# Lightning attention: the mixing product on the full array, with a block-diagonal matrix that VectorE writes in two parts

## The chip, the core and the metric

The kernel runs on one core of a Trainium2 chip. The metric is the time of one execution on the device, in microseconds (us), as the median of several runs. The core has a matrix engine (TensorE; PE in the profile, and PEld for its weight loads, which overlap the products), VectorE (DVE), ScalarE (ACT), GpSimd (POOL), and SyncE (SP), which issues the DMAs of this kernel. TensorE multiplies a stationary matrix (the weights, at most 128 rows by 128 columns) by a moving one that streams through it.

## The reference

Two decoder layers run on 2048 tokens (32 sequences of 64) of width 256. The change touches one of their six blocks, the lightning attention of the second layer, cut here to what is computed for each of 16 heads:

```python
qkv = silu(x @ w_qkv.T)                     # split into q, k, v of 128 each
for each block of 32 tokens, in order:
    o_inter = (q * q_decay) @ kv
    o_intra = ((q @ k.T) * diag_decay) @ v
    kv = block_decay * kv + (k * k_decay).T @ v
out = norm_w * out * rsqrt(mean(out * out) + eps)
return (sigmoid(x @ w_gate.T) * out) @ w_out.T
```

A sequence has 64 tokens only, so for each sequence and head this is one 64x64 matrix: the scores q k^T times a decay that is zero above the diagonal, applied to v. The kernel computes it in that form.

## The kernel before

`build` runs the blocks of both layers one after the other, with a barrier between stages. `lightning_attention` first normalises the tokens (`layernorm`, which leaves them split into a high and a low half-precision part, `xh` and `xl`), and then runs 64 steps: 16 heads (h) times four blocks (q) of 512 tokens, or eight sequences. In a step s the work is this:

- TensorE (the function under `@block.tensor`, `pair`): `wide` makes Q and K of the next step (6 products of 512 columns each, into banks 0 and 1). Then come the **scores** of this step (L1867): for each of the four tiles of 128 tokens (two sequences) and each of its two halves r, one product of k and q of the same sequence, in full precision, 128 rows by 64 columns of the array, 64 columns streamed, into bank 4. Then `wide` for the gate of the next step, `output` of the step before (12 products of 256 columns, from `yh` and `yl`), the **mixing** (L1880), and `values` of the next step (24 products of 128 columns). The mixing has eight products in full precision: the values `vS` of one sequence as weights (64 rows by 128 columns, so half of the array's rows), and the masked scores of that sequence `A[half[r], j, :]`, 64 columns, streamed. Half r writes to bank 4 + r, columns 256 to 511.
- VectorE: `mask` multiplies the scores in bank 4 by the decay and writes `A` (L1758, one instruction of 128x256), `add` sums the output of the step before from banks 6 and 7 into `ACC` (L1769), `gated` makes y (L1775) and, after ScalarE's `yh`, its low part `yl` (L1778). In the first step of each head `weights_low` (L1626) stands between `add` and `gated`.
- ScalarE: takes Q, K, gate and values out of their banks, copies the result of the mixing into `oS` (L1725, from both banks), and makes `yh` (L1732). GpSimd sums the squares of `oS`, and splits the weights of a later block.

The order on each engine is written out by hand, and semaphores join them: `scored` and `masked` between TensorE and VectorE, `mixed` and `ocopied` between TensorE and ScalarE. The scores wait for `ocopied` of the step before, because bank 4 holds a part of the mixing's result. `prep` lets ScalarE begin, and TensorE after it, once VectorE has prepared its constants (L1748 to L1752). Each full-precision product appears in the trace as two weight loads and two products, so the eight of a step are 16 rows.

Of the kernel before, what the change touches and what calls it, by code (L numbers as in the profile page):

```python
# [20 lines left out]
ALU = mybir.AluOpType  # L21
ACT = mybir.ActivationFunctionType
AX = mybir.AxisListType.X
ds = bass.ds

BATCH, SEQ, D = 32, 64, 256
TOK = BATCH * SEQ
P = 128
# [4 lines left out]
TPB = BLK // P  # L33
# [547 lines left out]
def gqa_cross_attention(nc, m, w, W):  # L581
# [13 lines left out]
    with ExitStack() as own:  # L595
# [22 lines left out]
        NLOAD = 1 + 2 + 1 + 1 + 3 + 2  # L618
        NPREP = 1 + KC * C + 1
        def preload(sp):  # L620
# [853 lines left out]
class KeptWeights:  # L1474
# [24 lines left out]
    def parts(self, h):  # L1499

        A, B, D2 = self.views(self.WS[:, :])[h]
        return ((A, self.W13[:, :, :, 0:P]), (B[:, :, :, 0:self.FB], self.W13[:, :, :, P:]), (D2, self.W2[:, :, :]))

# [37 lines left out]
def lightning_attention(nc, m, w, KW):  # L1541
# [18 lines left out]
    with ExitStack() as own:  # L1560
        def sb(n, s, dt=F32):
            return m.sb("d_" + n, s, dt, own)
# [7 lines left out]
        tri = sb("tri", [P, SEQ])  # L1570
        decay = sb("decay", [P, NH, SEQ])
        qT, kT, gt, vS, oS = (sb(n, [P, 2, BLK]) for n in ("qT", "kT", "gt", "vS", "oS"))
        A = sb("A", [P, TPB, SEQ])
        half = [slice(r * SEQ, (r + 1) * SEQ) for r in range(2)]
        y = sb("y", [P, BLK])
        yh, yl = (sb(n, [P, BLK], F16) for n in ("yh", "yl"))
# [4 lines left out]
        eps = sb("eps", [P, 1])  # L1581
        sd = sb("sd", [P, NT])
        rstd = sb("rstd", [P, NT])
        NPREP = 4
        EVENLY, LATELY = 2, [(0, 1), (0, 3), (1, 1)]

        def flat(x):
# [42 lines left out]
        with nc.Block() as block:  # L1630
# [45 lines left out]
            @block.scalar  # L1676
            def _(act):
                act.wait_ge(prep, NPREP)
                act.sem_inc(evac, 4)  # L1679
                act.sem_inc(ocopied, 1)  # L1680
                act.sem_inc(squared, 4)

                def weights_high(h):

                    act.wait_ge(wload, 48 * h + 48)
                    act.wait_ge(wt_in, 16 * h)
                    act.activation(flat(Ws[:, 0]), flat(Wn[:, :, :]), ACT.Copy, scale=SPLIT).then_inc(whigh, 1)

                def qk(s, q):
                    for n, dst in enumerate((qT, kT)):  # L1690
                        act.wait_ge(proj, 4 * s + n + 1)
                        act.activation(dst[:, q % 2, :], m.bank[n][:, :], ACT.Silu, scale=UNSPLIT).then_inc(evac, 1)

                def gate(s, q):
                    act.wait_ge(proj, 4 * s + 3)
                    act.activation(gt[:, q % 2, :], m.bank[2][:, :], ACT.Tanh, scale=0.5 * UNSPLIT).then_inc(evac, 1)

                def values(s, q):
                    act.wait_ge(proj, 4 * s + 4)
                    act.activation(vS[:, q % 2, :], m.bank[3][:, :], ACT.Silu, scale=UNSPLIT).then_inc(evac, 1)  # L1700

                def root(tiles):
                    act.wait_ge(ssq, tiles.stop // TPB)
                    act.activation(sd[:, tiles], m.bank[0][:, tiles], ACT.Sqrt, scale=UNSCALE / (NH * HD),
                                   bias=eps[:, :]).then_inc(sd_ready, 1)

                def pair(i, last):
                    for st in range(SPP):
                        u, q = divmod(st, SPH)
                        s, h = i * SPP + st, i * 2 + u  # L1710
                        end = last and st == SPP - 1
                        if not end:
                            qk(s + 1, q + 1)
                            if q == 0 and not (last and u == 1):
                                weights_high(h + 1)
                            if last and (u, q) in LATELY:
                                KW.scalar(act, NH - 2 + LATELY.index((u, q)))
                            elif not last and q == EVENLY:
                                KW.scalar(act, h)
                            gate(s + 1, q + 1)  # L1720
                        else:
                            root(slice(0, NT - TPB))
                        act.wait_ge(squared, 2 * s + 2)
                        act.wait_ge(mixed, s + 1)
                        act.activation(oS[:, q % 2, :].rearrange("p (j r t) -> p j r t", j=TPB, r=2),  # L1725
                                       m.psum[:, 4:6, 256:512].rearrange("p r (j t) -> p j r t", j=TPB),
                                       ACT.Copy).then_inc(ocopied, 1)
                        if not end:
                            values(s + 1, q + 1)
                        act.wait_ge(yready, s + 1)  # L1730
                        m.wait_apart(act, outs, s + 1)
                        act.activation(yh[:, :], y[:, :], ACT.Copy, scale=nw[:, ds(h, 1)]).then_inc(yhigh, 1)  # L1732
                        if end:
                            root(slice(NT - TPB, NT))

                for h in range(NH):
                    act.activation(decay[:, h, :], rel[:, :], ACT.Exp, scale=slope[:, h:h + 1]).then_inc(decays, 1)
                qk(0, 0)
                gate(0, 0)
                values(0, 0)  # L1740
                act.sem_inc(outs, 1)
                with act.Fori(0, PAIRS - 1) as i:
                    pair(i, False)
                pair(PAIRS - 1, True)

            @block.vector
            def _(dve):
# [2 lines left out]
                dve.wait_ge(loaded, 16 * 4)  # L1750
                dve.tensor_scalar(nw[:, :], nw[:, :], 0.5 * YS, None, ALU.mult).then_inc(prep, 1)
                dve.tensor_scalar(slope[:, :], slope[:, :], -1.0, None, ALU.mult).then_inc(prep, 1)  # L1752
                dve.sem_inc(masked, 1)
                dve.sem_inc(summed, 1)

                def mask(s, h):
                    dve.wait_ge(scored, s + 1)
                    dve.tensor_tensor(A[:, :, :], m.bank[4][:, 0:256].rearrange("p (a b) -> p a b", a=TPB),  # L1758
                                      decay[:, ds(h, 1), :].broadcast_to((P, TPB, SEQ)), ALU.mult).then_inc(masked, 1)

                def add(s, q, fresh):
                    dve.wait_ge(outs, s + 2)
# [51 lines left out]
            def _(pe):  # L1814
# [35 lines left out]
                def pair(i, first, last):  # L1850
                    for st in range(SPP):
                        u, q = divmod(st, SPH)
                        s, h = i * SPP + st, i * 2 + u
                        end = last and st == SPP - 1
                        nslot, nq = ((st + 1) // SPH) % 2, (q + 1) % SPH
                        if not end:
                            if nq == 0:
                                pe.wait_ge(wt_in, 16 * (h + 2))
                            wide(s + 1, nq, nslot, Q)
                            wide(s + 1, nq, nslot, K)  # L1860
                        pe.wait_ge(evac, 4 + 4 * s + 2)
                        pe.wait_ge(masked, s + 1)
                        pe.wait_ge(ocopied, s + 1)
                        for j in range(TPB):
                            for r in range(2):
                                tok = slice(j * P + r * SEQ, j * P + (r + 1) * SEQ)
                                mm = pe.matmul(m.bank[4][half[r], j * SEQ:(j + 1) * SEQ], kT[:, q % 2, tok], qT[:, q % 2, tok],  # L1867
                                               start=True, stop=True)
                        mm.then_inc(scored, 1)
                        if not end:  # L1870
                            wide(s + 1, nq, nslot, GT)
                        else:
                            square_sums(range(SPH - 1))
                        if not (first and st == 0):
                            output(s - 1, (st - 1) % SPP // SPH)
                        pe.wait_ge(masked, s + 2)
                        pe.wait_ge(evac, 4 + 4 * s + 4)
                        for j in range(TPB):
                            for r in range(2):
                                mm = pe.matmul(m.bank[4 + r][:, 256 + j * SEQ:256 + (j + 1) * SEQ],  # L1880
                                               vS[half[r], q % 2, j * P:(j + 1) * P], A[half[r], j, :], start=True, stop=True)
                        mm.then_inc(mixed, 1)
                        if not end:
                            values(s + 1, nq, nslot)
# [402 lines left out]
def experts_top4(nc, m, w, KW, rows_dram, y_dram, out):  # L2287
# [20 lines left out]
    with ExitStack() as own:  # L2308
# [25 lines left out]
        with nc.Block() as block:  # L2334
# [179 lines left out]
            def _(pe):  # L2514
                def hidden(s, weights, rows):
# [4 lines left out]
                    for j in range(len(weights)):  # L2520
                        tok, (A, B) = slice(j * BLK // len(weights), (j + 1) * BLK // len(weights)), weights[j]
                        for bank, W in ((0, lambda x, k: A(x, k, 0)), (1, lambda x, k: A(x, k, 1)), (2, B)):
# [148 lines left out]
```

## Time and profile before

| | us |
|---|---|
| median of 3 runs | 2389.93 |
| lowest and highest of them | 2388.23, 2400.44 |
| the profiled execution, its own time | 2389.24 |
| its span, from first to last instruction | 2387.4 |
| mean granted TensorE clock | 0.769 |
| lightning attention's 64 steps, first to last mixing | 651.3 to 1179.3 |

Three kinds of view are read below. A table of stretches gives each engine's busy time in a piece of the span, with the TensorE clock that was granted (1.00 is full speed, 2.4 GHz, and 0.50 is 1.2 GHz). Groups of instructions give count, busy time and mean duration. The timeline lists instructions in order of time, with like ones merged: a row with x16 and 1.11 us is sixteen instructions, from the start of the first to the end of the last. The recorded duration of a product holds the way through the array too, so the pace of a row is read from starts: its length less the duration of one, divided by the count less one.

### The profile page before, as it was taken

What the parts mean: (1) busy time and instruction counts of PE and PEld (TensorE: products, weight loads), DVE (VectorE), ACT (ScalarE), POOL (GpSimd) and SP (SyncE); (2) the same over time, 40 slices, a digit from 0 to 9 for tenths busy, and PEclk for the clock granted to TensorE, in tenths of its full rate; (3) what the DMA queues carried; (4) which work ended last, traced back from release to release, by engine and by line L of the source; (5) the groups of instructions that cost most, each with busy time, mean ns of one, the idle gap of its engine ahead of it and who ended that gap; (6) DMA issues with size and microseconds to landing.
All of it is one profiled execution on the core that took longest, in us unless ns stands there. A gap on an engine that the chain in (4) does not pass through costs nothing. (4 is left out here: it accounts for less than half of the span.)

```text
span 2387.4 us, 43105 instructions
## 1 busy us (share of the span) xinstructions
PE 1657.3 (69%) x15916; PEld 1021.4 (43%) x15916; DVE 1641.9 (69%) x2837; ACT 1285.0 (54%) x1770; POOL 1184.8 (50%) x1087
## 2 busy tenths in 40 slices
PE   6874595288499999999874566666666654178761
PEld 3332364265266666666563122222222223157640
DVE  5999477435545555555587899999999984634344
ACT  4664485032355555555432788888888871045430
POOL 0000284244234444444434688888888880055436
PEclk9997798599699999999987555555555557589985
DMA  3000221484322332222100466565556551688844
GB/s 106 1 0 0 54 75 40 101 201 118 72 80 66 86 82 67 74 76 75 54 27 0 76 107 109 106 110 105 108 107 107 107 98 35 230 190 211 167 110 131
DMA packets 506355, 219.08 MB, mean 92 GB/s; under 512 B 425485, under 2 KB 493653, under 8 KB 506197
## 3 DMA queue, kind: packets, MB, share of 16 engines
q1 hardware_dynamic: 494677, 185.47, 34.9%
q0 software_dynamic: 11520, 31.47, 5.5%
q8 instruction: 103, 1.69, 0.3%
q14 instruction: 55, 0.45, 0.1%
HBM read 79.87 MB, written 36.31 MB: 49 GB/s over the span
## 5 line engine op out<-in xcount | busy, mean ns | idle before, releaser
L2140 POOL CAST xnT<-xl 128x2048 bf16<-128x2048 uint8 x256 | 483.5, 1889 | 15.3
L2178 PE MATMUL psum<-e_KT,e_QT 48*128 48x512 bf16 x1024 | 265.0, 617 | 251.3 <-DVE ctxT L2211 124.7
L2211 DVE TENSOR_SCALAR_CACHE_REDUCE ctxT<-psum,e_nsq 128x1024 f32<-128x1024 f32 x256 | 314.7, 1282 | 7.9 <-PE psum L2178 6.5
L2211 DVE TENSOR_SCALAR_CACHE_REDUCE e_Smore<-psum,e_nsq 128x1024 f32<-128x1024 f32 x256 | 314.7, 1282 | 1.7 <-issue 0.4
L2229 ACT ACTIVATE xh<-ctxT,e_ebias 128x2048 uint8<-128x2048 f32 x128 | 256.2, 2002 | 53.6 <-POOL e_ebias L2147 53.6
L2229 ACT ACTIVATE xh<-e_Smore,e_ebias 128x2048 uint8<-128x2048 f32 x128 | 256.2, 2002 | 42.4 <-POOL e_ebias L2147 42.4
L1653 POOL TENSOR_TENSOR d_sq<-d_oS 128x512 f32<-128x512 f32 x60 | 93.4, 1557 | 273.6 <-ACT d_oS L1725 273.6
L120 PE MATMUL psum<-xh,d_T 128*128 128x512 f16 x768 | 220.2, 382 | 5.1 <-ACTq L1679 5.1
L2178 PEld LDWEIGHTS psum<-e_KT,e_QT 48*128 48x128 bf16 x1024 | 33.9, 107 | 381.2 <-DVE ctxT L2211 190.0
L661 POOL TENSOR_TENSOR b_bias<-b_alibi,b_neg 128x1024 f32<-128x1024 f32 x16 | 37.8, 2366 | 277.5 <-DVE b_Vbd L760 277.5
L2392 POOL DMA_INDIRECT xnT<-kept_rows,f_token x96 | 95.0, 989 | 153.1 <-DVE f_token L1135 68.6
L2188 PEld LDWEIGHTS psum<-e_Vi,xnT 128*128 128x128 bf16 x4096 | 119.6, 105 | 112.2 <-issue 91.0
L1769 DVE TENSOR_TENSOR d_ACC<-psum,d_ACC 128x512 f32<-128x512 f32 x120 | 77.3, 686 | 129.9 <-PE psum L120 129.9
L2188 PE MATMUL psum<-e_Vi,xnT 128*128 128x16 bf16 x4096 | 131.4, 175 | 7.4 <-POOL xnT L2140 7.4
L120 PE MATMUL psum<-f_Z,f_W 128*128 128x256 f16 x864 | 107.0, 287 | 41.5 <-DMA f_Z<-xnT 38.5
L1778 DVE SCALAR_TENSOR_TENSOR d_yl<-d_y,d_nw,d_yh 128x512 f16<-128x512 f32 x64 | 83.6, 1306 | 74.3 <-ACT d_yh L1732 74.3
L120 PE MATMUL psum<-xl,d_T 128*128 128x512 f16 x384 | 115.1, 382 | 0.0
L120 PEld LDWEIGHTS psum<-f_Z,f_W 128*128 x864 | 86.8, 102 | 60.8 <-issue 46.6
L2147 POOL TENSOR_SCALAR e_ebias<-e_mn 128x1 f32<-128x1 f32 x256 | 73.3, 286 | 64.0 <-DVE ctxT L2211 28.6
L2555 PE MATMUL psum<-f_W,f_hh 128*128 (+1 forms) x448 | 71.0, 286 | 41.9 <-DVE f_hh L2458 36.8
L2412 ACT ACTIVATE f_Z<-psum 128x512 f32<-128x512 f32 x28 | 16.7, 597 | 152.5 <-PE psum L120 152.5
L120 PEld LDWEIGHTS psum<-xh,d_T 128*128 128x128 f16 x768 | 67.6, 98 | 71.8 <-issue 7.7
(387 smaller groups left out, 3971.4 us busy)
## 6 DMA issues: line engine op xcount, KB each, us to landing
kept_y<-ctxT SPq DMA_DIRECT2D x24, 512.0 KB, 4.6
kept_w<-k_WS SPq DMA_DIRECT2D x17, 640.0 KB, 3.5
f_W<-kept_w SPq DMA_DIRECT2D x17, 640.0 KB, 11.5
kept_y<-c_y SPq DMA_DIRECT2D x12, 512.0 KB, 4.6
d_Wn<-in_L_attn_w_qkv SPq DMA_DIRECT2D x16, 384.0 KB, 3.5
k_W<-in_L_ffn_w_routed SPq DMA_DIRECT2D x32, 176.0 KB, 3.7
kept_rows<-xnT SPq DMA_DIRECT2D x8, 512.0 KB, 3.5
xl<-xh SPq DMA_TRANSPOSE x256, 3.0
```

The costliest lines, as they stand in the source:

```text
L120: mm = pe.matmul(out, lhsT(a, k), rhs(b, k), start=(n == 0), stop=(n == len(terms) - 1))
L1653: pool.tensor_tensor(sq[:, :], o, o, ALU.mult).then_inc(squared, 1)
L1769: last = dve.tensor_tensor(a2, m.bank[6 + half][:, :], a2, ALU.add)
L1778: dve.scalar_tensor_tensor(yl[:, :], y[:, :], nw[:, ds(h, 1)], yh[:, :], ALU.mult, ALU.subtract).then_inc(ysplit, 1)
L2140: pool.tensor_copy(PT[:, sl, :], P8[:, sl, :, :].rearrange("p c q -> p (c q)").bitcast(U8)).then_inc(unpacked, 1)
L2147: pool.tensor_scalar(ebias[:, sl:sl + 1], mn[:, sl, 0:1], mn[:, sl, 1:2], LN255, ALU.min, ALU.add).then_inc(biased, 1)
L2178: mm = pe.matmul(m.bank[pair_banks(c + odd) + q], QT[rows, n // 2, :], KTt[rows, n % H // 2, col:col + BLK], start=True, stop=True)
L2188: mm = pe.matmul(m.bank[6 + j // 8][:, j % 8 * HD:(j % 8 + 1) * HD], PT[:, n % SLOTS, k // 2 * 2 * P + k % 2:(k // 2 + 1) * 2 * P:2], Vi[: ...
L2211: dve.tensor_scalar(S32[sl][:, hf * HALF:(hf + 1) * HALF].rearrange("p (a b) -> p a b", a=2), m.psum[:, b:b + 2, :], nsq[:, n + odd:n + od ...
L2229: act.activation(e8[:, sl, :], S32[sl], ACT.Exp, bias=ebias[:, sl:sl + 1], scale=-1.0, accum_out=esum[:, n:n + 1]).then_inc(exped, 1)
L2392: pool.indirect_dma_start(got[:, qd % GOT, j, :], None, rows_dram[:, :], bass.IndirectOffsetOnAxis(R.token[:, i:i + 1], 0)).then_inc(fetch ...
L2555: mm = pe.matmul(m.bank[y_bank(s) + j // 2][:, (j % 2) * D:(j % 2 + 1) * D], a, b, start=(n == 0), stop=(n == len(terms) - 1))
```

## The change

`A` becomes 128 columns wide for each tile (`[P, TPB, P]`). Its two off-diagonal blocks are set to zero once, before the first step (two more instructions counted in `prep`, so NPREP is 6). `mask` writes the two diagonal blocks, in two instructions of 64 partitions each. The mixing is four products of 128x128 by 128 columns instead of eight on half the rows, all into bank 5, and ScalarE copies that one bank. TensorE's wait for `ocopied` moves from ahead of the scores to ahead of the mixing. The scores stay as they are.

```diff
-        A = sb("A", [P, TPB, SEQ])
+        A = sb("A", [P, TPB, P])
...
-        NPREP = 4
+        NPREP = 6
...
-                        act.activation(oS[:, q % 2, :].rearrange("p (j r t) -> p j r t", j=TPB, r=2),
-                                       m.psum[:, 4:6, 256:512].rearrange("p r (j t) -> p j r t", j=TPB),
-                                       ACT.Copy).then_inc(ocopied, 1)
+                        act.activation(oS[:, q % 2, :], m.bank[5][:, :], ACT.Copy).then_inc(ocopied, 1)
...
+                for rows, other in (half, half[::-1]):
+                    dve.memset(A[rows, :, other], 0.0).then_inc(prep, 1)
...
                 def mask(s, h):
                     dve.wait_ge(scored, s + 1)
-                    dve.tensor_tensor(A[:, :, :], m.bank[4][:, 0:256].rearrange("p (a b) -> p a b", a=TPB),
-                                      decay[:, ds(h, 1), :].broadcast_to((P, TPB, SEQ)), ALU.mult).then_inc(masked, 1)
+                    for rows in half:
+                        ins = dve.tensor_tensor(A[rows, :, rows], m.bank[4][rows, 0:256].rearrange("p (a b) -> p a b", a=TPB),
+                                                decay[rows, ds(h, 1), :].broadcast_to((SEQ, TPB, SEQ)), ALU.mult)
+                    ins.then_inc(masked, 1)
...
                         pe.wait_ge(evac, 4 + 4 * s + 2)
                         pe.wait_ge(masked, s + 1)
-                        pe.wait_ge(ocopied, s + 1)
                         for j in range(TPB):
...
                         pe.wait_ge(masked, s + 2)
                         pe.wait_ge(evac, 4 + 4 * s + 4)
+                        pe.wait_ge(ocopied, s + 1)
                         for j in range(TPB):
-                            for r in range(2):
-                                mm = pe.matmul(m.bank[4 + r][:, 256 + j * SEQ:256 + (j + 1) * SEQ],
-                                               vS[half[r], q % 2, j * P:(j + 1) * P], A[half[r], j, :], start=True, stop=True)
+                            tok = slice(j * P, (j + 1) * P)
+                            mm = pe.matmul(m.bank[5][:, tok], vS[:, q % 2, tok], A[:, j, :], start=True, stop=True)
                         mm.then_inc(mixed, 1)
```

On TensorE, in the second step of the stage, the order around the mixing was this (`d_yh` and `d_yl` are the output's operands, `d_A` and `d_vS` the mixing's, `d_T` with `xh` or `xl` the values'; the size is the moving operand's, or that of the result's tile):

```order
 L120 MATMUL psum<-d_T,d_yh 128x256 x2
 L120 MATMUL psum<-d_T,d_yl 128x256
-L1880 MATMUL psum<-d_A,d_vS 128x64 [waits b_maxed,b_exped]
-L1880 MATMUL psum<-d_A,d_vS 128x64 x7
+L1882 MATMUL psum<-d_A,d_vS 128x128 [waits b_pt,b_maxed,b_exped]
+L1882 MATMUL psum<-d_A,d_vS 128x128 x3
 L120 MATMUL psum<-d_T,xh 128x128 [waits b_maxed]
 L120 MATMUL psum<-d_T,xh 128x128 x3
```

Eight products with 64 columns each have become four with 128, the neighbours on both sides are the same, and the mixing's first instruction has a third wait. (The names of semaphores are those of an earlier stage that used the same ones: `b_pt` is `ocopied`.)

On VectorE, at the start of the stage and in its first step, before:

```order
478 L1748 MEMSET d_ones 128x1
479 L1749 MEMSET d_eps 128x1
480 L1751 TENSOR_SCALAR d_nw<-d_nw 128x16
481 L1752 TENSOR_SCALAR d_slope<-d_slope 128x16
482 L1801 TENSOR_TENSOR d_decay<-d_decay,d_tri 128x1024
483 L1758 TENSOR_TENSOR d_A<-psum,d_decay 128x256
484 L1626 SCALAR_TENSOR_TENSOR d_Ws<-d_Wn,d_Ws 128x1280
```

The same place now:

```order
478 L1746 MEMSET d_ones 128x1
479 L1747 MEMSET d_eps 128x1
480 L1749 TENSOR_SCALAR d_nw<-d_nw 128x16
481 L1750 TENSOR_SCALAR d_slope<-d_slope 128x16
482 L1752 MEMSET d_A 64x4x64 x2
483 L1803 TENSOR_TENSOR d_decay<-d_decay,d_tri 128x1024
484 L1759 TENSOR_TENSOR d_A<-psum,d_decay 64x4x64 x2
485 L1626 SCALAR_TENSOR_TENSOR d_Ws<-d_Wn,d_Ws 128x1280
```

Two memsets stand ahead of ScalarE's release, and each mask is two instructions; nothing else has moved.

## Rows read from the trace of the kernel before

**Rows 1.** A stretch: PE, PEld, DVE, ACT, POOL busy (count), clock, DMA share, GB/s.

```profile
900.00:1000.00 100.00, 100.00 (x1030) 67.32 (x1030) 50.87 (x64) 53.56 (x90) 44.22 (x33) 1.00 0.29 77
```

**Rows 2.** Who waited for whom, TensorE, 640 to 1190: total us, times, longest.

```profile
PE psum L120 <- DVE d_yl L1778: 3.1, 1, 3.1
```

**Rows 3.** Timeline of TensorE, 902.9 to 905: start, us, engine, line, names, count.

```profile
902.87 0.38 PE L120 MATMUL psum<-d_T,d_yh 128*128 128x256 f16 x2
903.09 0.27 PE L120 MATMUL psum<-d_T,d_yl 128*128 128x256 f16 x1
903.29 1.11 PE L1880 MATMUL psum<-d_A,d_vS 64*128 64x64 f32 x16
904.33 0.40 PE L120 MATMUL psum<-d_T,xh 128*128 128x128 f16 x4
...
903.29 0.97 PEld L1880 LDWEIGHTS psum<-d_A,d_vS 64*128 64x128 f32 x16 [0.21 <-issue]
```

**Rows 4.** The next step's mixing, and one line's durations (ns, minimum/median/maximum), TensorE.

```profile
911.69 1.11 PE L1880 MATMUL psum<-d_A,d_vS 64*128 64x64 f32 x16
...
L1880 PEld LDWEIGHTS psum<-d_A,d_vS x1024: 182/188/188, 651.3 to 1180.1; 64*128 64x128 f32 x171
L1880 PE MATMUL psum<-d_A,d_vS x1024: 272/272/320, 651.3 to 1180.1; 64*128 64x64 f32 x171
```

**Rows 5.** Full-array full-precision weight loads, timeline of TensorE in the last step.

```profile
1175.19 2.84 PE L1847 MATMUL psum<-d_ones,d_SQ 128*128 128x1 f32 x24
1177.89 0.38 PE L120 MATMUL psum<-d_T,d_yh 128*128 128x256 f16 x2
...
1175.19 2.75 PEld L1847 LDWEIGHTS psum<-d_ones,d_SQ 128*128 128x128 f32 x24
```

**Rows 6.** Full-array products of other stages, timeline of TensorE.

```profile
346.29 1.04 PE L816 MATMUL psum<-ident,b_S 128*128 128x128 f32 x8
...
1219.63 2.75 PE L2080 MATMUL psum<-e_Wkv,ctxT 128*128 128x256 f32 x12
...
1240.21 0.62 PE L2092 MATMUL psum<-e_identb,e_Tk 128*128 128x128 bf16 x8 [0.17 <-POOL e_Tk L1980]
1240.66 0.87 PE L2080 MATMUL psum<-e_Wq,xnT 128*128 128x256 f32 x3
...
1240.61 0.19 PEld L2080 LDWEIGHTS psum<-e_Wq,xnT 128*128 128x128 f32 x1
```

**Rows 7.** VectorE groups: busy us, mean ns, idle us before and releaser.

```profile
L1758 DVE TENSOR_TENSOR d_A<-psum,d_decay 128x256 f32<-128x256 f32 x64 | 27.0, 422 | 28.6 <-PE psum L1867 28.6
...
L2449 DVE TENSOR_TENSOR f_Z<-psum,f_Z 48x512 f32<-48x512 f32 x28 | 19.5, 695 | 0.9
L2447 DVE TENSOR_TENSOR f_Z<-psum,f_Z 128x512 f32<-128x512 f32 x28 | 19.4, 691 | 107.6 <-ACT f_Z L2412 107.5
```

**Rows 8.** Timeline of VectorE around the start of a head, and TensorE's next output.

```profile
920.20 1.29 DVE L1769 TENSOR_TENSOR d_ACC<-psum,d_ACC 128x512 f32<-128x512 f32 x2 [2.16 <-PE psum L120]
921.41 1.48 DVE L1626 SCALAR_TENSOR_TENSOR d_Ws<-d_Wn,d_Ws 128x1280 f16<-128x1280 f32 x1
...
925.41 0.75 DVE L1778 SCALAR_TENSOR_TENSOR d_yl<-d_y,d_nw,d_yh 128x512 f16<-128x512 f32 x1 [1.07 <-ACT d_yh L1732]
...
927.09 0.38 PE L120 MATMUL psum<-d_T,d_yh 128*128 128x256 f16 x2
...
L1778 DVE SCALAR_TENSOR_TENSOR d_yl<-d_y,d_nw,d_yh x64: 750/1595/1597, 655.1 to 1182.7; 128x512 f16<-128x512 f32 x64
```

**Rows 9.** The stage's start: timeline of VectorE, GpSimd, TensorE, and a memset elsewhere.

```profile
636.57 2.09 DVE L1752 TENSOR_SCALAR d_slope<-d_slope 128x16 f32<-128x16 f32 x1
...
638.55 0.57 POOL L1506 MEMSET k_W<- 128x512 f32 x1
...
638.86 0.58 PE L120 MATMUL psum<-xh,d_T 128*128 128x512 f16 x1 [5.14 <-ACTq L1679]
...
L336 DVE MEMSET a_pad<- 96x192 f32 x1 | 0.2, 218 | 2.6 <-PEq L179 2.6
```

## The prediction

> **What bounds the kernel now.** Only the lightning attention changes, so I read its stretch alone. The table of stretches comes first [rows 1]: in 100 us of it TensorE is busy for all 100, at full clock, while VectorE has 51, ScalarE 54 and GpSimd 44. The view of who waited for whom [rows 2] confirms it: from 640 to 1190 us TensorE's products waited for another engine once that it shows, for 3.1 us, at the stage's end. The timeline gives the period: mixings start at 903.29 and 911.69, so a step takes 8.40 us [rows 3, 4], and 62 of the 63 spacings are the same (the last, without a next step's products, is shorter). So TensorE alone sets the time of the 64 steps, and what the change does to TensorE's own sequence is what it does to the kernel, as long as the others keep up.
>
> How long does the mixing take there? The last product before it starts at 903.09 and the first after it at 904.33 [rows 3]. The three output products from 902.87 stand 0.11 apart, so the last would have made room after 0.11. The mixing's slot is 904.33 - 903.09 - 0.11 = 1.13 us. Inside it, the weight loads come in pairs, one for each half of the rows, and their row is 0.97 us for 16 of 0.188 [rows 3, 4]: (0.97 - 0.19) / 7 = 0.111 us per pair. The streaming of 64 columns is shorter than that and lies under the loads: the pace is that of loading 128 columns of full-precision weights, 8 pairs x 0.111 = 0.89. The other 0.24 are the edges: 0.09 before the first load (903.29 against 903.20), and what lies between the last product, which starts at 903.29 + 1.11 - 0.27 = 904.13, and 904.33, of which its pair's own streaming is the smaller part. TensorE stands empty while it goes over to half arrays, and again while it comes back.
>
> **TensorE's mixing after the change.** Four products of two weight loads each make 8 loads in place of 8 pairs. The trace has such loads on the full array, those of the square sums: 24 loads and products, whose load row is 2.75 us with 0.19 for one, (2.75 - 0.19) / 23 = 0.111 [rows 5]. So a full load costs what a pair of half ones did. New is that each load's product streams 128 columns, twice as many. Full-precision products of 128 columns come at (1.04 - 0.27) / 7 = 0.11 [rows 6], but these are transposes, with a cheaper load; products of 256 columns come at (2.75 - 0.38) / 11 = 0.215, and their loads, which are of the expensive kind, hide entirely [rows 6]. So load and product run side by side, and with both at 0.11 the pace should be 0.112: 8 x 0.112 = 0.90 us.
>
> The edges go. From a 16-bit product to full precision on the full array the trace shows products at 1240.66 and a load at 1240.61, directly behind the last one of L2092: that row ends at 1240.83 and one lasts 0.22, so the last starts at 1240.61 too, and no empty time lies between [rows 6]. On the way back, the 24 products from 1175.19 to 1177.89 take 2.70 / 24 = 0.1125 each, the step to the output's first 16-bit product included [rows 5]. Here the mixing's first load has a 256-column output product of 0.11 to hide under. So the slot is 0.90 in place of 1.13, and from the unrounded starts I take 0.238 us per step; 64 x 0.238 = **15.2 us less**. Bounds: a pace of 0.109 instead of 0.112 gives 0.262, or 16.8; a first load that doesn't hide costs 0.107 per step, which leaves 0.131, or 8.4. I take 15.2, since the row at 1240.61 shows the load going ahead.
>
> The Trainium skill, in "TensorEngine Tiling (Array Packing)", section Key Properties, says that changing the tiling mode drains TensorE; by that rule both edges are drains and the change removes two of the four per step. The trace agrees, with 0.09 us ahead of the mixing.
>
> **The waits.** The wait for `ocopied` goes from the scores to the mixing. The copy that it asks for belongs to the step before, and is 7 us old by then; nothing is queued behind it that it holds. The scores lose a wait that never held either. TensorE's queue reads such waits ahead, as it did at 1240.61, where a load with a wait of its own directly follows L2092's last product [rows 6].
>
> **VectorE's mask.** Time goes by elements per partition and not by partitions: 48x512 took 695 ns and 128x512 691 [rows 7]. So each half of the mask costs the 422 ns of the whole one [rows 7], and VectorE has 64 x 0.42 = 27 us more work. It is hidden where the mask stands: VectorE was idle for the 2.16 us between the mask and `add` at 920.20 [rows 8], and the mixing that needs `A` starts at 903.29 + 2 x 8.40 = 920.09, 2.05 us after the mask's end. Without that cover it would cost 0.42 per step.
>
> **What is late next.** The tightest place is `yl` in a head's first step, where `weights_low` (1.48 us) stands behind `add`: it ends at 925.41 + 0.75 = 926.16, and TensorE needs it at 927.09, so 0.93 is left [rows 8]. `add` starts when the output is ready, and a mixing shorter by 0.24 brings the next output nearer by as much: 0.69 stays. But `yl` takes 0.75 or 1.6 us [rows 8], by what GpSimd does beside it. Should it fall on the long one there, 0.85 - 0.69 = 0.16 us would be missing in 15 steps, 2.4 us at most. Nothing at the low end. I take 0.
>
> **The stage's start.** ScalarE, and after it TensorE (638.86), wait for VectorE's constants, which end at 636.57 + 2.09 = 638.66 [rows 9]. Two memsets of 256 elements per partition are added there; one of 192 took 218 ns [rows 9], so about 0.27 each, 0.5 us in all, once. If GpSimd's memset (638.55 to 639.12) held them up [rows 9], it would be 1.0; 0 if they ran into each other. I take 0.5.
>
> **Sum.** 0.5 - 15.2 = -14.7. The profiled execution took 2389.24 (its span 2387.4 and 1.84 around it), which gives 2374.5, and a span of 2372.7. The median of the runs shown stands 0.7 above it, at 2389.93: 2375.2. The period of a step is 8.16 in place of 8.40. The later stages begin after a barrier and should only move forward; I allow them 2 us either way, about what the two lower runs differ by.
>
> **Rivals.**
> 1. Load and product don't overlap when both are 0.11 long (slower). For: no row shows an expensive load with a product of 128 columns. Against: in half arrays and under 256 columns they overlap entirely. Then each of the 8 costs 0.107 more, at worst: 8 x 0.107 - 0.238 = +0.62 per step, 40 us, 2430. It decides from a pace of 1.13 / 8 = 0.142 us per load: above that the change loses.
> 2. Two half products at once are worth more than I say (slower). What half arrays save is streaming: 8 pairs of 64 columns against 8 of 128. One 64-column pass pair is half of the 0.107, so 0.43 us per step would be lost if streaming set the pace on both sides, 27 us, 2417. Against it stands the pace of 0.111 per pair, which is twice what 64 columns need [rows 3, 4]. The Trainium skill has this as a rule, in "TensorE: Matmul & The Clock Gate", section Packing small matmuls: products with few rows, put into different row groups, run at once, and that is their gain. By it alone the change would be a loss.
> 3. The edges stay (no change). If the empty time came from going between 16-bit and full precision, or from the waits, and not from half arrays, both would stay, and the mixing's inner part is as long as before: 0.5 us more at the start, 2390.5. Against it stand both edges of [rows 5, 6].
> 4. The first load doesn't hide: -8.4 + 0.5, 2382.
> 5. The change doesn't do what it says because VectorE takes TensorE's place as the bound: at 51 of 100 busy plus 5 it is far from that; it could only be the place named above, +2.4, which is 2377.6 and in the forecast's own range.
>
> **How the numbers follow.** Forecast (2371 to 2380) 0.79; first load exposed 0.07; edges stay 0.05; no overlap 0.05; streaming sets the pace 0.03; something below 2371 0.01. The range reaches from 2371 to the exposed load, 2382, and leaves out 0.14. A measurement of this kernel tells 0.5%, 12 us, from no change, so the border is 2378: faster by more is the forecast but for a small part of it where the start, `yl` and the later stages add up, 0.76; within 0.5% are that part, the exposed load and the edges, 0.16; slower 0.08.
>
> **What would show it.** Right: mixings 8.16 us apart; the mixing's product row eight strong and about 0.8 us from its first start to its last; nothing empty at either side, with the first product 0.11 behind the last output product; each mask two rows of 0.42; TensorE's idle before `d_yh` as before; TensorE's first product of the stage at about 639.4. Wrong: loads at over 0.12 us (rival 1 or 2); 0.09 and more ahead of the mixing (3 or 4); TensorE idle on `d_yl` in the second step of each head (`yl` late); a later stage that took back more than 2 us.

## The result, and the profile after

| | before | after |
|---|---|---|
| median of 13 runs each, taken side by side, us | 2398.05 | 2379.80 |
| lowest of them | 2386.53 | 2374.46 |
| ratio, with its 95% interval | | 0.9939 (0.9918 to 0.9961) |
| profiled execution, its own time | 2389.24 | 2379.82 |
| its span | 2387.4 | 2378.0 |

The change makes the kernel 0.6% faster: 14.6 us by the ratio, with 9 to 20 as its interval. The medians lie further apart, 18.3 us; the ratio is that of the means, in which one run of before, 2484.98 in a slower state, is left out. A second comparison on another occasion, with six runs of the changed kernel and 17 of the one before, gave 0.9932 (0.9916 to 0.9948). The medians themselves sit higher than the three runs of before that stood ahead of the prediction: over 13 runs before is at 2398, not at 2390.

The stretch of the same length as in [rows 1], then TensorE's waits in the stage from its first products on, as in [rows 2], both of the changed kernel:

```profile
900.00:1000.00 100.00, 100.00 (x967) 69.78 (x965) 58.96 (x77) 55.42 (x94) 45.34 (x33) 1.00 0.28 77
...
PE psum L120 <- DVE d_yl L1780: 3.1, 1, 3.1
PE psum L120 <- ACT d_qT L1692: 0.7, 1, 0.7
```

TensorE is still busy for all 100 us at full clock, and is still the only bound; VectorE has gone from 51 to 59. The 3.1 us at the stage's end are what they were. The 0.7 us, once and at the start of the stage, don't stand in the first trace of before, but they are not the change's: the third trace of before has such a wait of 0.3, and the third of after has none. They go with the moment at which the clock rises, which the section on the start takes up. The timeline of TensorE around a mixing answers to [rows 3] (the mixing is L1882 now):

```profile
900.08 0.38 PE L120 MATMUL psum<-d_T,d_yh 128*128 128x256 f16 x2
900.29 0.27 PE L120 MATMUL psum<-d_T,d_yl 128*128 128x256 f16 x1
900.30 0.97 PEld L1882 LDWEIGHTS psum<-d_A,d_vS 128*128 128x128 f32 x8
900.40 1.06 PE L1882 MATMUL psum<-d_A,d_vS 128*128 128x128 f32 x8
...
901.30 0.39 PE L120 MATMUL psum<-d_T,xh 128*128 128x128 f16 x4
...
908.55 1.06 PE L1882 MATMUL psum<-d_A,d_vS 128*128 128x128 f32 x8
```

The first load starts with the last output product (900.30 against 900.29), so it lies under it; the first product of the mixing is 0.11 behind that one, where it was 0.20; eight loads take 0.97, which is (0.97 - 0.19) / 7 = 0.111 each; and the values' products begin 0.90 after the mixing's first, where it was 1.04. The next mixing starts at 908.55, 8.15 us later, where it was 8.40. Of the 0.25 us, 0.09 went ahead of the mixing, 0.15 inside it and at its back, and 0.01 in the first of the values' products.

VectorE in a head's first step answers to [rows 8]:

```profile
914.32 0.86 DVE L1759 TENSOR_TENSOR d_A<-psum,d_decay 64x256 f32<-64x256 f32 x2 [0.39 <-PE psum L1868]
916.90 1.29 DVE L1771 TENSOR_TENSOR d_ACC<-psum,d_ACC 128x512 f32<-128x512 f32 x2 [1.73 <-PE psum L120]
918.11 1.48 DVE L1626 SCALAR_TENSOR_TENSOR d_Ws<-d_Wn,d_Ws 128x1280 f16<-128x1280 f32 x1
919.51 1.53 DVE L1777 SCALAR_TENSOR_TENSOR d_y<-d_gt,d_oS 128x512 f32<-128x512 f32 x1
922.12 0.75 DVE L1780 SCALAR_TENSOR_TENSOR d_yl<-d_y,d_nw,d_yh 128x512 f16<-128x512 f32 x1 [1.08 <-ACT d_yh L1730]
```

The mask is two instructions and 0.86 us long, and 1.73 us of idle time are still left between it and `add`. `yl` keeps its short form here.

### The profile page after: what moved, and what is told of

It reads as the page before. It is cut to its first block and busy times, and to the rows that moved or that the text cites. A ratio compares the mean times of both kernels' runs of the same rounds, so it can differ in the third digit from the quotient of the medians.

```text
span 2378.0 us, 42208 instructions
## 1 busy us (share of the span) xinstructions
PE 1652.0 (69%) x15404; PEld 1027.5 (43%) x15404; DVE 1673.6 (70%) x2903; ACT 1286.5 (54%) x1770; POOL 1188.3 (50%) x1087
```

## Is the mask really free?

> The kernel before with one edit: the mask is written by two instructions of 64 partitions, as in the change, while the mixing stays on half arrays. Theory (VectorE's extra 0.42 us lies under TensorE's products): 128 mask instructions of 0.42 us, mixings still 8.40 us apart, time as before within 0.5%. Rival (VectorE's cover is gone somewhere, so the change paid for its mask and would have gained more without it): a step of 8.40 to 8.82, up to 27 us slower.

```diff
                 def mask(s, h):
                     dve.wait_ge(scored, s + 1)
-                    dve.tensor_tensor(A[:, :, :], m.bank[4][:, 0:256].rearrange("p (a b) -> p a b", a=TPB),
-                                      decay[:, ds(h, 1), :].broadcast_to((P, TPB, SEQ)), ALU.mult).then_inc(masked, 1)
+                    for rows in half:
+                        ins = dve.tensor_tensor(A[rows, :, :], m.bank[4][rows, 0:256].rearrange("p (a b) -> p a b", a=TPB),
+                                                decay[rows, ds(h, 1), :].broadcast_to((SEQ, TPB, SEQ)), ALU.mult)
+                    ins.then_inc(masked, 1)
```

Measured: ratio to before 0.9991 (0.9970 to 1.0011). In its trace, one mask of VectorE and two mixings of TensorE:

```profile
907.13 0.86 DVE L1759 TENSOR_TENSOR d_A<-psum,d_decay 64x256 f32<-64x256 f32 x2 [0.37 <-PE psum L1869]
...
901.32 1.11 PE L1882 MATMUL psum<-d_A,d_vS 64*128 64x64 f32 x16
...
909.72 1.11 PE L1882 MATMUL psum<-d_A,d_vS 64*128 64x64 f32 x16
```

The mask costs 0.42 us more and the step stays at 8.40. So VectorE's part of the change is free, and what the step gained came from TensorE's own sequence.

## What sets the pace of the mixing: load or streaming?

Two runs of the changed kernel alter how many columns each product of the mixing streams, and neither computes the right result. The first leaves out half of each output tile, and besides the line shown it zeroes bank 5 once, ahead of the first step. The second writes overlapping pieces. Each ran once, so its trace is what counts.

> The changed kernel, whose mixing streams only the first 64 of A's 128 columns per product (the other half of each output tile is left out, so half of the result isn't computed; the bank is zeroed once). Theory (the loading of full-precision weights sets the pace, 0.112 us per load, and streaming lies under it): the mixing still takes 8 x 0.112, the step 8.10 to 8.15. Rival 2 (streaming sets the pace on the full array): each of 8 passes 0.053 shorter, a step of 7.72, 27 us less over the stage.

```diff
-                            mm = pe.matmul(m.bank[5][:, tok], vS[:, q % 2, tok], A[:, j, :], start=True, stop=True)
+                            mm = pe.matmul(m.bank[5][:, j * P:j * P + SEQ], vS[:, q % 2, tok], A[:, j, 0:SEQ], start=True, stop=True)
```

> The changed kernel, whose mixing streams 192 columns per product instead of 128, into overlapping pieces of the bank (a wrong result, the same number of products). Theory (load and streaming run side by side, the longer one sets the pace): 192 columns need 0.160 us, so the pace is 0.162, the mixing 1.30 instead of 0.90, the step 8.55, which is 0.15 above the kernel before: the break-even pace is 0.142. Rival 1 (load and streaming add): 0.27 per pass, a step of 9.4.

```diff
+                            cols = slice(min(j * P, BLK - 192), min(j * P, BLK - 192) + 192)
-                            mm = pe.matmul(m.bank[5][:, tok], vS[:, q % 2, tok], A[:, j, :], start=True, stop=True)
+                            mm = pe.matmul(m.bank[5][:, cols], vS[:, q % 2, tok], A[:, :, :].rearrange("p a b -> p (a b)")[:, cols],
+                                           start=True, stop=True)
```

Timeline of TensorE, first of the run with 64 columns, then of the one with 192; in each the mixing, the product behind it, and the next mixing:

```profile
900.91 1.00 PE L1883 MATMUL psum<-d_A,d_vS 128*128 128x64 f32 x8
901.75 0.39 PE L120 MATMUL psum<-d_T,xh 128*128 128x128 f16 x4
...
909.01 1.00 PE L1883 MATMUL psum<-d_A,d_vS 128*128 128x64 f32 x8
```

```profile
906.84 1.47 PE L1883 MATMUL psum<-d_A,d_vS 128*128 128x192 f32 x8
908.14 0.39 PE L120 MATMUL psum<-d_T,xh 128*128 128x128 f16 x4
...
915.39 1.47 PE L1883 MATMUL psum<-d_A,d_vS 128*128 128x192 f32 x8
```

With half the columns the mixing takes 0.84 in place of 0.90 and the step is 8.10 (8.097 as the median of all): only the last product's own streaming is saved, the seven others come at the pace of their loads. With half as many again it takes 1.30, or 0.163 per pass, and the step is 8.56, above the kernel before. So both go side by side, the longer one counts, and at 128 columns the two are of nearly one length. That refutes rival 2, for which 64 columns would have given 7.72, and rival 1, for which 192 would have given 9.4; and it puts the change on the good side of the break-even pace of 0.142.

## What are the edges?

Two runs put one more product ahead of the mixing, on half of the rows or on all of them. Its result is overwritten. Each ran once.

> The changed kernel with one further product on half of the rows (64x128 by 64 columns) just ahead of the mixing, its result overwritten. Theory (the edges belong to going over to half arrays and back): 0.09 to go over, 0.05 of load laid bare, 0.11 for the second load, 0.20 to the mixing's first product and 0.11 for its load, which can't be pulled ahead any more: 0.56 us more than the change's 8.15, a step of 8.71. Rival 3 (the edges come with full precision or with the waits): 0.22 more, a step of 8.37.

```diff
+                        pe.matmul(m.bank[5][:, 0:SEQ], vS[half[0], q % 2, 0:P], A[half[0], 0, 0:SEQ], start=True, stop=True)
                         for j in range(TPB):
                             tok = slice(j * P, (j + 1) * P)
```

> The companion of the run with a further product on half of the rows: the same further product, 64 columns streamed, but on all 128 rows. Theory: two more loads of 0.112 and no edge, 0.22 us more than the change's 8.15, a step of 8.37; what the half-array product costs beyond that is the price of going over and back. Rival (any further full-precision product ahead of the mixing costs the same 0.56): 8.71.

```diff
+                        pe.matmul(m.bank[5][:, 0:SEQ], vS[:, q % 2, 0:P], A[:, 0, 0:SEQ], start=True, stop=True)
```

Timeline of TensorE, half of the rows first, then all rows:

```profile
907.93 0.27 PE L120 MATMUL psum<-d_T,d_yl 128*128 128x256 f16 x1
908.14 0.43 PE L1880 MATMUL psum<-d_A,d_vS 64*128 64x64 f32 x2
908.50 1.16 PE L1883 MATMUL psum<-d_A,d_vS 128*128 128x128 f32 x8
909.49 0.39 PE L120 MATMUL psum<-d_T,xh 128*128 128x128 f16 x4
```

```profile
907.51 0.27 PE L120 MATMUL psum<-d_T,d_yl 128*128 128x256 f16 x1
907.62 0.33 PE L1880 MATMUL psum<-d_A,d_vS 128*128 128x64 f32 x2
907.79 1.11 PE L1883 MATMUL psum<-d_A,d_vS 128*128 128x128 f32 x8
908.74 0.39 PE L120 MATMUL psum<-d_T,xh 128*128 128x128 f16 x4
```

The weight loads, half of the rows first, show when each could begin:

```profile
908.14 0.29 PEld L1880 LDWEIGHTS psum<-d_A,d_vS 64*128 64x128 f32 x2 [0.21 <-issue]
908.50 0.97 PEld L1883 LDWEIGHTS psum<-d_A,d_vS 128*128 128x128 f32 x8
```

```profile
907.52 0.30 PEld L1880 LDWEIGHTS psum<-d_A,d_vS 128*128 128x128 f32 x2
907.74 0.97 PEld L1883 LDWEIGHTS psum<-d_A,d_vS 128*128 128x128 f32 x8
```

From the last output product to the values' first it is 1.56 us with the half product and 1.23 with the full one, against 1.01 without either. The periods are 8.71 and 8.37, as the theory had them. The half product starts 0.21 behind the output, the full one 0.11, and the full one's load begins 0.01 behind that output's start, while the half one's waits until its product's: same data type, same waits, same bank, same neighbours. So the empty time comes neither from full precision nor from the waits, which was rival 3, but from going to half of the rows and back, and a single such product costs 0.33 us more than a full one. This shows the price of leaving the full array; that TensorE empties itself on the way is the Trainium skill's account of it ("TensorEngine Tiling (Array Packing)", Key Properties), and the 0.10 us by which the half product starts later agree.

## Would the scores gain by it too?

> The changed kernel with the scores on the full array too: four products of 128x128 by 128 columns, of which the mask takes the diagonal blocks. Theory (a full load costs 0.112, whether needed or not): the scores' weights are 64 columns wide, so their half-array loads cost only 0.058 per pair, 0.71 us for the slot with both edges; on the full array it is 8 x 0.112 = 0.90, a step of 8.15 + 0.18 = 8.33, 12 us slower than the change and 4 us faster than before. Rival (leaving half arrays always pays, the edges being what costs): a step below 8.15.

```diff
-                            for r in range(2):
-                                tok = slice(j * P + r * SEQ, j * P + (r + 1) * SEQ)
-                                mm = pe.matmul(m.bank[4][half[r], j * SEQ:(j + 1) * SEQ], kT[:, q % 2, tok], qT[:, q % 2, tok],
-                                               start=True, stop=True)
+                            tok = slice(j * P, (j + 1) * P)
+                            mm = pe.matmul(m.bank[4][:, tok], kT[:, q % 2, tok], qT[:, q % 2, tok], start=True, stop=True)
```

The mask reads the diagonal blocks of the scores out of bank 4 accordingly (that line isn't shown).

Timeline of TensorE: the last product of K, the scores on the full array, the gate's first, and the next scores:

```profile
903.01 0.59 PE L120 MATMUL psum<-xh,d_T 128*128 128x512 f16 x2
903.44 1.05 PE L1867 MATMUL psum<-d_qT,d_kT 128*128 128x128 f32 x8
904.33 0.59 PE L120 MATMUL psum<-xh,d_T 128*128 128x512 f16 x2
...
911.76 1.05 PE L1867 MATMUL psum<-d_qT,d_kT 128*128 128x128 f32 x8
```

The scores take 0.89 us from first start to the next product, and the step 8.32, 0.17 more than the change (0.18 expected). The edges did go: the first product starts 0.22 behind K's last, which is what a product of 512 columns takes. It didn't help: on half arrays the scores' weights are 64 columns wide and their row of 16 products is 0.69 us long, against 1.05 for the 8 here, whose loads are 128 columns wide. That costs more than the edges did. The ratio to before, 0.9984 (0.9965 to 1.0004), can't be told from no change, though the trace's period is 0.08 shorter than before's. Against the change itself it is slower: 2396.38 as the median, where the changed kernel had 2383.14 on the same occasion. Rival and theory differ in sign here, and the sign is the theory's.

## The start of the stage

> The changed kernel with the two memsets taken out of the chain that releases ScalarE and TensorE (they stand on VectorE behind it, ahead of the first mask). Theory: TensorE's first product of the stage comes 0.4 us earlier relative to the end of VectorE's constants, the steps stay 8.15 apart, and the time is the change's less 0.4 us, too little for the timing to tell: ratio to before 0.993 to 0.995.

```diff
-        NPREP = 6
+        NPREP = 4
...
-                for rows, other in (half, half[::-1]):
-                    dve.memset(A[rows, :, other], 0.0).then_inc(prep, 1)
                 dve.sem_inc(masked, 1)
                 dve.sem_inc(summed, 1)
+                for rows, other in (half, half[::-1]):
+                    dve.memset(A[rows, :, other], 0.0)
```

The start in the changed kernel's trace, VectorE and TensorE, as in [rows 9], and then in this run's:

```profile
641.26 2.09 DVE L1750 TENSOR_SCALAR d_slope<-d_slope 128x16 f32<-128x16 f32 x1
643.08 0.69 DVE L1752 MEMSET d_A<- 64x256 f32 x2
...
643.96 1.01 PE L120 MATMUL psum<-xh,d_T 128*128 128x512 f16 x2 [5.54 <-ACTq L1679]
```

```profile
643.73 2.09 DVE L1750 TENSOR_SCALAR d_slope<-d_slope 128x16 f32<-128x16 f32 x1
645.54 0.67 DVE L1754 MEMSET d_A<- 64x256 f32 x2
...
646.01 1.01 PE L120 MATMUL psum<-xh,d_T 128*128 128x512 f16 x2 [5.13 <-ACTq L1679]
```

In the change, TensorE starts 643.96 - 641.26 = 2.70 us after `d_slope` began, here 2.28, and in the kernel before 2.29: the memsets cost 0.41 us, and moving them gives it back at this place. The total doesn't show it: ratio 0.9942 (0.9927 to 0.9957). Nor does the trace a few steps on. From TensorE's first product to the first mixing it is 12.53 us here and 11.95 in the first trace of the change, which is 0.58 more and outweighs the 0.41. Two stretches of each, the changed kernel's first, cut where the clock changes (the last three columns are clock, DMA share and GB/s):

```profile
644.00:646.50 2.50, 2.50 (x7) 0.83 (x8) 0.00 (x0) 2.47 (x6) 0.00 (x0) 0.50 0.53 141
646.70:652.00 5.30, 4.63 (x40) 2.77 (x39) 1.23 (x1) 5.27 (x15) 0.00 (x0) 1.00 0.17 48
```

```profile
646.00:651.40 5.40, 5.38 (x13) 1.88 (x14) 0.28 (x2) 5.29 (x18) 0.28 (x1) 0.50 0.41 112
651.60:656.00 4.40, 4.40 (x40) 2.74 (x39) 0.96 (x1) 3.69 (x6) 0.00 (x0) 1.00 0.00 0
```

The clock went from 1.2 to 2.4 GHz 2.7 us after TensorE's first product in the one and 5.5 us after it in the other. So this start depends on when the clock rises by more than on the memsets. The first trace of before had its rise after 5.1 us, and 12.44 us to the first mixing. The stage with the late memsets was even 1.5 us longer than the change's first one: 0.2 of that had come up by the first mixing, and the rest came at the end, which the last section takes up. Nothing in the runs is measurably better than the changed kernel.

## The level of the other stages

> The changed kernel once more, on the chip that the others use, for its level and for a second trace of it. Theory: the stage alone changes, 16 us less for 64 steps and 0.4 more at its start, so the ratio to before is 0.9935, and what the first trace showed ahead of and behind the stage (4 to 5 us later there, 2 to 3 us given back behind) is the wander of the other stages and comes out otherwise in this trace. Rival (the change itself makes the stages around it slower, by where things lie in memory or by the clock): the same 4 to 5 us ahead of the stage, and a ratio of 0.996.

> The kernel before once more, for its trace. What is open: the first trace of it reached the stage at 636.5 us and spent 1195.6 us behind it, against 641 to 645 and 1197 to 1204 in the traces of the changed kernel and its relatives. Theory (other stages wander, and the first trace of before was a short one): this one reaches the stage at 641 to 645 and spends 1196 to 1203 behind it; the stage itself takes 555.3 again. Rival (the change lengthens what lies behind it): 1195 to 1197 behind it.

> The same kernel again, a third trace of it: the same expectations, 641 to 645 ahead of the stage and 1196 to 1203 behind it by the theory of wander, 1195 to 1197 behind it by the rival, and 555.3 in the stage.

> The changed kernel for a third trace, beside the two further ones of before: 539.4 us in the stage, with a period of 8.15; ahead of and behind the stage it lies among those of before by the theory of wander, and 2 to 4 us above them behind the stage by the rival.

Each trace cut in three, us: up to VectorE's first instruction of the stage, from there to the start of its last one in it, and the rest.

| trace | ahead | stage | behind |
|---|---|---|---|
| before, first | 636.5 | 555.3 | 1195.6 |
| before, second | 639.8 | 555.5 | 1187.7 |
| before, third | 641.1 | 556.5 | 1190.5 |
| mask in two | 643.1 | 555.1 | 1196.0 |
| after, first | 641.1 | 539.4 | 1197.4 |
| after, second | 644.8 | 539.4 | 1199.7 |
| after, third | 646.3 | 541.3 | 1193.8 |
| late memsets | 643.6 | 540.9 | 1200.8 |

The second and third traces of before and the third of after are from one occasion; the second of after and the late memsets share another.

The stage is the steady part: pair by pair it is 15.9, 16.1 and 15.2 us shorter after the change. The third traces, 556.5 and 541.3, lie above the 555.3 and 539.4 that I had expected while their periods are the same; the clock at the stage's two ends makes the difference. What lies around it is not steady. The same kernel spends 1188 to 1196 us behind it, and reaches it at 636 to 641. My figures for the two further traces of before were wrong on both theories (I had said 1196 to 1203, or 1195 to 1197, and got 1187.7 and 1190.5), and 639.8 ahead of the stage lies below the 641 to 645 that I named.

The traces of after didn't come out as the theory of wander had it either. The second should have lost the lag ahead of the stage and had 644.8, more than the first; the third should have lain among those of before and had 646.3 ahead, above all of them. Behind the stage all three lie above the second and third of before. Ahead of the stage the program is the same, and the run with the mask in two, whose `A` is as wide as before's, reached the stage at 643.1; so a gap of some us there can be wander. Behind it the matter is open. The nine traces of kernels with the wide `A`, those of the altered mixings and scores included, spend 1193.8 to 1203.8 us there, 1199.3 as the mean, and the four with the narrow one 1187.7 to 1196.0, mean 1192.5. Taken on the same occasion, the gap is 3 to 6 us: 1196.0 with the mask in two against 1199.2 to 1199.4 for the three runs beside it, and 1187.7 and 1190.5 against 1193.8.

The timings can't tell that from nothing. Their 0.9939 and 0.9932 agree with the stage's own 15.9 us (0.9934), and the second interval, up to 0.9948, leaves out the rival's 0.996. But a gain of 15.9 less 3 is a ratio of 0.9946, and it lies inside both intervals. What stays open with it is why the three profiled executions of before, 2385 to 2390, sit at the low end of its timed ones, whose median was 2397 to 2402.

## Where the prediction was right, and where not

- **The bound.** TensorE alone sets the step: confirmed, with 100 of 100 us and an even period before and after.
- **The mixing.** 8 loads at 0.112, first load hidden, nothing empty at either side: confirmed to the row. The slot is 0.90, as worked out.
- **The size per step.** 0.238 was said, 0.250 came. Up to the values' first product the traces give 0.24, as worked out; the values' second product then follows 0.01 sooner too (0.056 us behind the first, where it was 0.066). That it is the way back from half arrays that had drawn out this first product is likely and not shown. It makes 0.8 us over 64 steps.
- **VectorE.** The mask is two times 0.42 under cover, `yl` was never late: 0 of the 2.4 us held in reserve. Its busy share rose by 8 of 100 where 5 was said, which cost nothing.
- **The start.** 0.5 was said, 0.41 came up to TensorE's first product. By the first mixing the moment at which the clock rises moves more than that (0.58 between two traces), which the prediction didn't have.
- **The sum.** -14.7 us was forecast, a ratio of 0.9938; the stage's own first traces give -15.9, of which some 0.4 is the clock's earlier rise in the one of after, and the timings 0.9939 and 0.9932.
- **The level.** This step failed. I carried the difference over to one number by "a median of 2389.93" and allowed the later stages "2 us either way, about what the two lower runs differ by". The highest of those three runs, 2400.44, was already the better witness: over 13 runs the median of before is 2398.05, 8.1 above the 2389.93, and the parts ahead of and behind the stage each move by 5 to 8 us among three traces of before. The term was mis-sized: 2 us should have been some 8. The changed kernel's median in the first comparison, 2379.80, is 4.6 above the 2375.2 that I named, and inside the range. That is luck: with before at 2398.05 my -14.7 gives 2383.4, outside, and only because the medians happened to lie 18.3 apart did it fall inside. In the second comparison the median is 2383.14, 8 above, outside.
- **The later stages.** That they "should only move forward", within 2 us, isn't shown: the traces fit 3 us given back behind the stage as well as wander, and no run decides.
- **The chance of faster by over 0.5%.** I gave it 0.76. The ratio's interval, 0.9918 to 0.9961, lies on both sides of 0.995, so the first comparison leaves it undecided; the second (0.9916 to 0.9948) is wholly below. With such a level a gain of 0.6% is harder to tell from 0.5% than I had allowed.

## What to carry to other kernels

Half-array products pay by their weight loads and their columns, and each excursion costs its edges. Count full-precision passes as the longer of load and streaming. Where the half product's weights are as wide as the full one's, and 64 columns stand against 128, as in the mixing, going to half arrays saves streaming that was hidden anyway and pays 0.24 us of edges for it. Where its weights are half as wide, as for the scores, it wins in spite of them. Other sizes weren't tried. And take the level of a prediction from the spread of the runs, not from the closest two.

## What the hardware showed that I had not expected

The end of the stage depends on the clock, and so does its start. In the last step TensorE makes 24 loads and products of one column each, the square sums, 2.7 us long. In five of the 13 traces the granted clock fell from 2.4 to 1.2 GHz by the end of these or within the output that follows, 2.5 to 3.6 us after they began, with TensorE busy up to then; in the eight others only once TensorE had stood idle behind the last mixing. The timeline of TensorE in the run with the late memsets, which is one of the five, then its stretches (their last three columns are clock, DMA share and GB/s):

```profile
1166.79 2.88 PE L1849 MATMUL psum<-d_ones,d_SQ 128*128 128x1 f32 x24
...
1171.30 1.91 PE L1882 MATMUL psum<-d_A,d_vS 128*128 128x128 f32 x8
...
1166.00:1169.00 3.00, 3.00 (x41) 2.83 (x38) 1.80 (x2) 2.49 (x3) 2.48 (x2) 1.00 0.03 9
1169.00:1171.00 2.00, 2.00 (x17) 1.74 (x18) 0.87 (x3) 0.27 (x1) 0.00 (x0) 0.84 0.00 0
1171.20:1173.00 1.80, 1.80 (x10) 1.72 (x8) 1.29 (x2) 0.00 (x0) 0.00 (x0) 0.50 0.00 0
```

The same place in the first trace of the changed kernel:

```profile
1164.15 2.88 PE L1849 MATMUL psum<-d_ones,d_SQ 128*128 128x1 f32 x24
...
1168.20 1.06 PE L1882 MATMUL psum<-d_A,d_vS 128*128 128x128 f32 x8
...
1168.00:1170.00 2.00, 1.25 (x12) 1.05 (x9) 1.31 (x3) 0.60 (x1) 0.00 (x0) 1.00 0.00 0
```

The last mixing took 1.91 us there and 1.06 here, with TensorE busy throughout in both. The third traces of before and after show it as well: their last two mixings are 7.90 and 7.54 apart, where 7.20 and 6.99 is the rule, and their stages are some 1 and 1.9 us longer than their siblings'. The other two of the five are the runs with 64 columns and with the scores on the full array. So the clock can fall while TensorE has work without a gap, and the same kernel shows it in one execution and not in another. This alone moves the end of the stage by 1 to 2 us. What brings it down is open: that it has to do with the square sums, which stream one column per load, is suggested by the place alone, and no run replaced them.
